# Layer-norm rows of a fused attention and expert block, moved from ScalarE to VectorE

## The reference

```
def layernorm(x): return (x - mean(x)) / sqrt(var(x) + 1e-5)      # over the 128 features
q = layernorm(x) @ Wq.T; k, v = ctx @ Wk.T, ctx @ Wv.T            # 16 heads
x = x + tanh(g_xattn) * (softmax(q k^T + mask) v) @ Wo.T
n = layernorm(x)
w = top-2 of softmax(n @ Wg + bg), scaled to sum 1
x = x + tanh(g_ffn) * sum_e w[e] * (relu(n @ W1[e] + b1[e]) @ W2[e] + b2[e])
```

## Time and profile before

| | |
|---|---|
| median of 3 runs | 1107.41 us (1107.24 to 1107.66) |
| the profiled execution's own time | 1107.66 us |
| its span in the profile | 1105.6 us |
| mean granted TensorE clock | 0.99 |
| busy, share of the span: TensorE | 93% |
| ScalarE | 85% |
| VectorE | 81% |
| GpSimd | 72% |

### The profile page before, as it was taken

One profiled execution on the slowest core, in us unless ns is written; L12 is line 12 of the kernel. 1 busy time (PEld: TensorE's weight loads), 2 busy tenths in 40 slices (PEclk: granted clock), 3 DMA queues, 4 the chain that ended last, 5 costly groups with the idle time before them and its releaser, 6 DMA issues.

```text
span 1105.6 us, 36301 instructions
## 1 busy us (share of the span) xinstructions
PE 1024.9 (93%) x13797; PEld 755.4 (68%) x13797; DVE 894.4 (81%) x1803; ACT 943.1 (85%) x1809; POOL 791.7 (72%) x719
## 2 busy tenths in 40 slices
PE   5868799999999999999999999999999999999887
PEld 4446567776777777677777767777776777777655
DVE  2686688897888889788888978888897888787766
ACT  3988788889898888989888898988889898887865
POOL 3566667776867777686777768777776877788843
PEclk9999899999999999999999999999999999999999
DMA  9122121212112121211212121121212111111100
GB/s 219 33 56 59 49 56 43 55 45 59 50 40 57 52 57 43 59 50 40 57 52 56 43 59 50 40 57 52 54 45 59 50 31 46 44 40 50 29 3 20
DMA packets 123162, 56.90 MB, mean 51 GB/s; under 512 B 26584, under 2 KB 122864, under 8 KB 122992
## 3 DMA queue, kind: packets, MB, share of 16 engines
q1 hardware_dynamic: 122992, 54.59, 19.3%
HBM read 16.80 MB, written 4.19 MB: 19 GB/s over the span
## 4 chain that ended last, share of the span: by engine, by line
PE 49%; DVE 14%; ACT 12%; issue 12%; POOL 11%; DMA 1%; ACTq 0%; DVEq 0%; SPq 0%; POOLq 0%
PE bank L44 15%; PE bank L46 14%; PE bank L45 14%; POOL hidL L895 3%; POOL ptL L932 3%; ACT qH L464 3%; POOL rstd L880 3%; PE bank L307 2%; ACT bank L520 2%; PE bank L262 2%; DVE shift L668 2%; ACT x2hat L508 1%; DVE comb L868 1%; ACT vH L559 1%; DVE above L844 1%
## 5 line engine op out<-in xcount | busy, mean ns | idle before, releaser
L895 POOL TENSOR_TENSOR hidL<-hid,hidH 128x512 f16<-128x512 f32 x242 | 278.6, 1164 | 21.3 <-ACT hidH L494 21.3
L932 POOL TENSOR_TENSOR ptL<-pt,ptH 128x512 f16<-128x512 f32 x128 | 148.5, 1160 | 179.4 <-ACT pt L579 179.4
L675 DVE TENSOR_TENSOR qL<-bank,qH 128x512 f16<-128x512 f32 x224 | 153.4, 685 | 57.1 <-ACT qH L464 53.7
L484 ACT ACTIVATE hid<-bank,b1col 128x512 f32<-128x512 f32 x256 | 185.6, 725 | 8.3 <-PE bank L46 8.2
L494 ACT ACTIVATE hidH<-bank,b1col 128x512 f16<-128x512 f32 x256 | 188.3, 736 | 0.0
L464 ACT ACTIVATE qH<-bank 128x512 f16<-128x512 f32 x256 | 155.1, 609 | 36.0 <-PE bank L46 35.0
L44 PE MATMUL bank<-w2H,hidH 128*128 128x128 f16 x1024 | 179.0, 220 | 5.8 <-DVE hidL L788 5.2
L46 PE MATMUL bank<-w2H,hidL 128*128 128x128 f16 x1024 | 179.1, 220 | 0.0
L45 PE MATMUL bank<-w2L,hidH 128*128 128x128 f16 x1024 | 179.1, 220 | 0.0
L927 POOL TENSOR_TENSOR x<-x,y_scaled 128x512 f32<-128x512 f32 x114 | 146.0, 1280 | 14.1 <-DVE x L746 14.1
L938 POOL TENSOR_TENSOR prob<-prob,row_inv 128x512 f32<-128x512 f32 x128 | 133.4, 1043 | 15.2 <-DVE row_inv L782 15.2
(11 more groups left out here) (143 smaller groups left out, 3607.3 us busy)
## 6 DMA issues: line engine op xcount, KB each, us to landing
vdH<-vH SPq DMA_DIRECT2D x256, 64.0 KB, 2.1
vdL<-vL SPq DMA_DIRECT2D x256, 64.0 KB, 2.1
x_raw<-in_x SPq DMA_DIRECT2D x16, 256.0 KB, 3.0
ctx_raw<-in_ctx SPq DMA_DIRECT2D x16, 256.0 KB, 3.1
mask_raw<-in_fside_Bx1xSxS SPq DMA_DIRECT2D x32, 128.0 KB, 2.8
out_x<-x SPq DMA_DIRECT2D x16, 256.0 KB, 2.5
qH<-in_L_xattn_Wq SPq DMA_DIRECT2D x1, 512.0 KB, 6.0
qH<-in_L_xattn_Wk SPq DMA_DIRECT2D x1, 512.0 KB, 8.1
```

The source lines that it names most:

```text
L484: act.activation(hid[:, k % NR, :], bk("hid", g, e, c)[:, :], ACT.Relu, bias=b1col[:, e, c:c + 1]).then_inc(s_relu[c], 1)
L675: dve.tensor_tensor(qL[at], bk("Q", g, h)[:, :].rearrange("p (b q) -> p b q", b=GB), qH[at], ALU.subtract).then_inc(s_q_low[h % 2], 1)
L895: pool.tensor_tensor(hidL[:, m % 2, c, :], hid[:, k % NR, :], hidH[:, m % 2, c, :], ALU.subtract).then_inc(s_hid_low[c], 1)
L932: pool.tensor_tensor(ptL[:, b % 2, :], pt[:, b % 2, :], ptH[:, b % 2, :], ALU.subtract).then_inc(s_pt_low, 1)
```

## The change

The rows are made by VectorE, by (x - mean) * rstd, with one `tensor_scalar` for each of the four tiles that takes both scalars from memory. They stand where `ln_shift` stood. `shift`, its tile and its semaphore go; ScalarE has no part in the layer norms any more.

```diff
-            def ln_rows(w, g, src, dst, freed):
-                act.wait_ge(s_ln[w]["shift"], g + 1)
-                if freed is not None:
-                    act.wait_ge(*freed)
-                for t in range(GT):
-                    last = act.activation(dst[:, t, :], src[:, t, :], ACT.Identity, bias=shift[:, w, t:t + 1],
-                                          scale=rstd[:, w, t:t + 1])
-                last.then_inc(s_ln[w]["rows"], 1)
...
-                if i == 5 - sooner and within(g + 2, GROUPS):
-                    ln_rows(0, g + 2, x_raw[:, (g + 2) % NX], xhat[:, :, :], (s_xT, g + 2))
-                if i == 5 and within(g - 1, GROUPS):
-                    ln_rows(1, g - 1, x2[:, (g - 1) % NX2], x2hat[:, :, :], (s_x2T, g - 1) if g >= 2 else None)
...
-            def ln_shift(w, g):
+            def ln_rows(w, g, src, dst, freed):
                 dve.wait_ge(s_rstd[w], g + 1)
-                if g:
-                    dve.wait_ge(s_ln[w]["rows"], g)
-                dve.scalar_tensor_tensor(shift[:, w], meanvar[:, w, :, 0], -1.0, rstd[:, w], ALU.mult,
-                                         ALU.mult).then_inc(s_ln[w]["shift"], 1)
+                if freed is not None:
+                    dve.wait_ge(*freed)
+                for t in range(GT):
+                    last = dve.tensor_scalar(dst[:, t, :], src[:, t, :], meanvar[:, w, t, 0:1], rstd[:, w, t:t + 1],
+                                             ALU.subtract, ALU.mult)
+                last.then_inc(s_ln[w]["rows"], 1)
...
                     if i == 5 - sooner:
-                        ln_shift(0, g + 2)
+                        ln_rows(0, g + 2, x_raw[:, (g + 2) % NX], xhat[:, :, :], (s_xT, g + 2))
...
                     if i == 5:
                         ln_var(1, g - 1)
-                        ln_shift(1, g - 1)
+                        ln_rows(1, g - 1, x2[:, (g - 1) % NX2], x2hat[:, :, :], (s_x2T, g - 1) if g >= 2 else None)
```

More of the change, by code:

```diff
@@ L80, in flamingo_block @@
         rstd = sb("rstd", [P, 2, GT])
-        shift = sb("shift", [P, 2, GT])
         minus_half = sb("minus_half", [P, GT])
@@ L167, in flamingo_block @@
         s_marked, s_mask_in = sem("score_banks_marked"), sem("mask_in_bank")
-        s_ln = [{k: sem(f"ln{w}_{k}") for k in ("stats", "aggr", "var", "shift", "rows")} for w in range(2)]
+        s_ln = [{k: sem(f"ln{w}_{k}") for k in ("stats", "aggr", "var", "rows")} for w in range(2)]
         s_logit_in, s_gt, s_eq, s_gmax, s_gshift = (sem(n) for n in ("logit_in", "gt", "eq", "gate_max", "gate_shift"))
@@ L522, in mask_into_bank @@
                                ACT.Copy, scale=WS).then_inc(s_mask_in, 1)
-            ln_rows(0, 0, x_raw[:, 0], xhat[:, :, :], None)
             for n in range(H // 4):
@@ L687, in _ @@
             ln_var(0, 0)
-            ln_shift(0, 0)
+            ln_rows(0, 0, x_raw[:, 0], xhat[:, :, :], None)
             for n in range(H // 4):
```

## The result

Twelve timed runs of the changed kernel gave a median of **1114.68 us** (1109.31 to 1120.30), twelve of the kernel before in the same session 1107.59 us. The ratio is 1.0069, with a 95% interval of 1.0048 to 1.0090: slower by 0.7%. The forecast was 1118.6 us. The profiled execution, a thirteenth, is one of the quickest: its own time is 1110.3 us, its span 1108.6, which is 3.0 more than before.

The account below looks back on a forecast made before the run. TensorE was taken as the bound, busy 62.48 of each 64.5 us period. Steady groups +22.8, groups 14 and 15 +2, ramp -12.6 and tail -1 gave +11.2 on 1107.66, less 0.25: 1118.6 us, range 1098 to 1127.

Parts of the forecast that it names:

- The place and the break-even: Step 6, first hidden product: VectorE may be 1.5 us later; each us beyond that is a us per group.
- T: Moment VectorE is through with the second layer norm: 512.31 before, break-even 513.80, forecast 515.7, 1.9 us beyond.
- T - Q: Time from the first query matmul of step 6 (Q) to VectorE being through with the second layer norm.
- The holds on VectorE: Steps 5 and 6: one VectorE instruction gets through between two GpSimd instructions; the next waits for a whole one.
- The fourth piece: Last `tensor_scalar` of `x2hat`: comes at about 514.6, is held 1.16 us by `ptL`, to 515.7.
- the first rival: Fourth `tensor_scalar` of `x2hat` slips in ahead of `ptL`: 0.6 us a group, 1103 us; chance 0.26.
- the term of +1.9 a group: Steady groups: VectorE 1.9 us beyond break-even in each of 12 groups, +22.8 us.
- The price of a free piece: Start-to-start time of a `tensor_scalar` that is not held: 0.2 us, bounds 0.16 and 0.26.
- The estimate of 0.19 from start to start: Two elements a cycle in fp32 would give 0.19 us instead of 0.26, with the same number of waits.
- The ramp: Groups -1, 0 and 1: ScalarE's holds and TensorE's slow clock go, -12.6 us, bounds -8 and -14.
- The rival that the ramp gives nothing: TensorE waits for VectorE in the ramp instead: +17, 1124 us; the forecast with it has chance 0.48.
- Groups 14 and 15 and the tail: Groups with only the second norm: about +1 each, +2 us; last norm at the end: -1 us (0 to -2).

Follow-up runs that it names:

- `x` cut short: Changed kernel with GpSimd's addition of `y_scaled` to `x2` in every step 6 cut to one column, leaving out part of the experts' sum: 1092.39 us, ratio 0.9861.
- second norm only: Kernel before with only the second norm's rows made by VectorE, the first norm's left on ScalarE: 1111.07 us, ratio 1.0033.
- constants: Changed kernel with constants 0.0 and 1.0 in place of the two scalars from memory, leaving out the layer norms; one run: 1098.22 us.
- first norm only: Kernel before with only the first norm's rows made by VectorE, the second norm's left on ScalarE: 1111.64 us, ratio 1.0028.
- eight pieces: Changed kernel with eight `tensor_scalar` of 64 columns in place of four of 128, for both norms: 1170.1 us, ratio 1.0562.
- behind the addition: Changed kernel with the second norm's rows moved to step 6, behind `y_scaled` and L722: 1090.68 us, ratio 0.9840.
- behind the second `qL`: Changed kernel with the second norm's rows moved behind the second `qL` of step 6: 1072.58 us, ratio 0.9683.
- on ScalarE later: Kernel before, rows on ScalarE; second norm's `shift` behind the addition to `x2` in step 6, its activations behind the second `qH`: 1087.72 us, ratio 0.9821.

## Why the prediction was near, and where it was off

**The place and the break-even.** Right. Four kernels whose streams are alike up to T put a line through the claim that each us of T beyond break-even is a us per group; T - Q and the period are read in the same steady group:

| | T - Q | period | period less 64.48 |
|---|---|---|---|
| `x` cut short | 3.94 | 64.20 | -0.28 |
| second norm only | 4.26 | 64.54 | +0.06 |
| constants | 4.41 | 64.70 | +0.22 |
| changed kernel | 4.91 | 65.22 | +0.74 |

Over 0.97 of T the period grows by 1.02. The line crosses zero at 4.20; the forecast put break-even at T - Q = 3.94. Most of these 0.26 lie between the first hidden product and the next query: 450.08 - 445.32 = 4.76 here, where the forecast had 4.93. The second hidden product follows the first by 1.45, as forecast (1.44); it is the stretch behind it that is 0.17 shorter. The first norm only lies off this line, with ScalarE's waits still in it.

**The holds on VectorE.** Right: one VectorE instruction gets through between two GpSimd instructions, and the next pays for a whole one. Pieces of 0.6, 1.2, 0.3, 0.3 were forecast for `xhat` and 0.68, 1.20, 0.33, 0.33 measured; of `x2hat` the first three, 1.1, 1.3 and 0.3, came as 1.19, 1.30 and 0.33. Relative to Q the root starts at 0.95 (0.89 forecast), `hidL` ends at 3.11 (3.04), the second piece at 4.41 (4.44). The short addition shows the hold's cause, the eight pieces that it counts instructions and not elements.

**The fourth piece: the step that failed.** The forecast had it held by `ptL`, T - Q = 5.84 and a wait of 3.4 us. It slips in, as the first rival had it, at 4.92, and the wait is 2.56. In the one steady group where it was held (at 641.5) T - Q is 642.79 - 636.77 = 6.02 and the wait 3.67: the price of the hold was right, the fork went the other way, by 0.15 us of issue time. So the term of +1.9 a group is +0.74. The rival's own T - Q was 4.54, 0.4 low. The price of a free piece, taken as 0.2 and measured as 0.26, makes 0.1 of that; the rest is a slip in its sum, which let T come 0.1 after the end of the second piece at 514.3 with two pieces still to run. Its 0.6 a group is near the measured 0.74 only because its break-even was 0.26 low too. That a price of 0.26, the upper bound, would hold the third piece did not come about either.

By the Trainium skill (VectorE: DVE Perf Modes, "Mode 2×_2P — use both read ports for one tensor") the form handles two fp32 elements a cycle. The runs agree: from 64 to 128 columns a piece grows from 0.302 to 0.333, 64 elements in 0.031 us. Between the forms with a PSUM input, L722 with 128 columns (0.33) and `qL` with 512 (0.67), 64 elements come to an estimated 0.057, about twice that. The estimate of 0.19 from start to start was too low all the same: 0.26 was measured. It began from L735, which has one scalar from memory, and the two of a piece cost 0.12.

**The clock: the missing term.** The sum charged a low clock only in the ramp. Behind the new waits it falls in some steady groups too, for about 1.6 us each. Of the thirteen executions, the profiled one has a mean granted clock of 0.993 and a span of 1108.6, three with 0.980 have 1118.0 to 1118.6, and the rest lie in near order (the shortest, 1107.6, has 0.989). The 0.013 are some 29 us at half clock, eight or nine such stretches, an estimated 13.6 us at 1.6 each where 10 were measured. That fits the median being 4.4 us above the profiled execution. The forecast had no such term, so it is luck that the median comes closer to it than its steps deserve. The kernels that bring the wait below 1 us (one of 2.1 apart; behind the addition, behind the second `qL`, on ScalarE later) show no fall in their steady groups. Why one group falls and the next does not, behind the same wait, is open.

**The ramp.** Right in sign: the clock is 1.00 through both windows of the earlier trace rows, and the waits of 4.24 and 5.76 are gone. Windows of the changed kernel, which is ahead of the one before and so at later work:

```profile
82.60:84.50 1.90, 1.90 (x17) 1.07 (x15) 1.90 (x5) 1.32 (x4) 1.90 (x3) 1.00 0.35 67
...
133.00:135.00 2.00, 2.00 (x34) 1.52 (x32) 1.71 (x3) 1.95 (x5) 0.51 (x1) 1.00 0.31 67
```

The size was nearer than its terms. From 20 us to the ramp's last common wait, in the kernel before and then in the changed one:

```profile
20.00:160.40 140.40, 112.10 (x1365) 76.76 (x1364) 101.46 (x204) 119.41 (x239) 83.62 (x75) 0.94 0.23 59
```
```profile
20.00:149.90 129.90, 107.34 (x1367) 75.47 (x1366) 108.25 (x216) 113.17 (x222) 83.69 (x75) 0.99 0.31 65
```

Of these 10.5 us, 5.7 are idle time of TensorE and 4.8 are busy time for the same matmuls, which is the clock. The forecast was -12.6: -9.9 of waits and -2.7 of clock. The waits came short because TensorE then waits twice at the transposition behind L722, 6.0 us together; the clock gave more, since only one fall of 3.4 us is left of 17. That the two partly cancel is luck, and the clock's part is that of one execution. The rival that the ramp gives nothing because these waits turn into VectorE's is half right for the waits.

**Groups 14 and 15 and the tail.** +2 and -1 were forecast; measured is -1.2 together. From transposition to transposition, groups 14 and 15 take 63.91 and 56.17 us, against 62.86 and 54.51 before: +2.7. The way to the last transposition is then 2.1 shorter (39.09 against 41.21), and what follows it 1.8 shorter; there the kernel before has a low clock of 3.4 us at 1079.7, some 1.6 us, which the changed one lacks. So the tail gave -3.9 where -1 was forecast; why the last norm gained 2.1 was not taken apart.

**What decides the sign.** Engine and place are two changes. On ScalarE but later the kernel gains 1.8%, on VectorE at the same late place 3.2%, on VectorE at the old place it loses 0.7%. The table of the three columns says where: place alone takes 709.5 to 693.2 in the eleven periods and leaves the first column at 196.0; engine on top of it takes the first column to 184.1 and the periods only to 691.4.

## What to carry to other kernels

Before work is added to an engine's stream, find the first instruction behind it that frees something for the bound engine, and set the work behind that, with the slack up to its consumer in view: here a place two instructions later was worth 24 us, and one six later 42. On VectorE beside a busy GpSimd count instructions and not elements, since each can cost a whole GpSimd instruction. Where a fork is decided by tenths, price both ways, and price the clock behind each new wait too.

## What the runs showed of the hardware

- A wait of 2.6 us on TensorE was followed by 3.4 us at 1.2 GHz in some groups and by none in others of the same run; with 1.9 us it fell twice in a run, with 2.05 us (constants) and 1.58 us (`x` cut short) in no steady group, and with 5.0 us (eight pieces) in every one, for 3.4 or 6.8 us.
- A `tensor_scalar` of 128x128 in fp32 takes 0.215 us with constants and 0.333 with two scalars from memory; with half the columns and two such scalars, 0.302. From one start to the next in a row of them it is 0.26 (two scalars, 128 columns).
- A VectorE instruction of four elements per partition (`rstd`, 1.20 in the earlier trace rows) is held as long as one of 128 (1.20 here, second piece of `xhat`).
